# Interleaving two panels on TensorE, with one landing ring of five slots and seven fixed turned slots

## The reference

```python
h = jnp.maximum(_layernorm(x, axis=-1), 0.0)
# the layer, on ego = h (first 2048 rows users, the rest items)
u = par_u[0] * par_u[1] * (diag_u[:, None] * ego_u @ W_u) + ego_u
i = par_i[0] * par_i[1] * (diag_i[:, None] * ego_i @ W_i) + ego_i
e = jnp.concatenate([u, i], axis=0)
h = adj @ (adj.T @ e)
out = (h - mean(h)) * rsqrt(var(h) + 1e-5) * ln_gamma + ln_beta + res   # res = ego
x = x + out
```

## Time and profile before

| | us |
|---|---|
| median of 3 runs | 540.03 (538.85 to 540.18) |
| the profiled execution, its own time | 538.86 |
| its span, first to last instruction | 537.0 |
| busy: TensorE matmul / VectorE / ScalarE / GpSimd | 445.0 / 343.5 / 312.5 / 26.9 |
| DMA: moved, mean rate | 139.43 MB, 260 GB/s |
| mean granted TensorE clock, share of full | 0.93 |

### The profile page before, as it was taken

How to read it: one execution, slowest core, us unless ns; L and a number is a source line. 1 busy time by engine, 2 the same in 40 slices (tenths; PEclk the granted TensorE clock), 3 DMA queues, 4 the chain that set the end, 5 groups by cost and what they waited for, 6 DMA issues and landing times.

```text
span 537.0 us, 5378 instructions
## 1 busy us (share of the span) xinstructions
PE 445.0 (83%) x2108; PEld 179.7 (33%) x2108; DVE 343.5 (64%) x338; ACT 312.5 (58%) x415; POOL 26.9 (5%) x30
## 2 busy tenths in 40 slices
PE   0747554599969989999969799997899898779996
PEld 0313222243423334324423333433343332334433
DVE  2635199473999941499991149999118999701742
ACT  2365830856699924069993207998324699622242
POOL 1011330000000000000000000000000000001132
PEclk9968795899979999999989899998999999799999
DMA  7966109685965979996957699795979968772911
GB/s 222 404 259 264 56 0 379 169 234 165 366 253 214 408 284 206 324 371 253 415 205 281 191 319 372 269 415 206 330 262 315 392 243 338 276 251 63 302 52 59
DMA packets 63112, 139.43 MB, mean 260 GB/s; under 512 B 4208, under 2 KB 37488, under 8 KB 63088
## 3 DMA queue, kind: packets, MB, share of 16 engines
q1 hardware_dynamic: 45360, 123.28, 63.1%
q10 hardware_dynamic: 17728, 15.82, 10.6%
HBM read 137.78 MB, written 1.31 MB: 259 GB/s over the span
## 4 chain that ended last, share of the span: by engine, by line
PE 29%; ACT 22%; DMA 22%; DVE 18%; issue 6%; ACTq 1%; SPq 1%; DVEq 0%
ACT ready L369 20%; DMA nat<-in_adj_dram 17%; PE tT_ps L673 11%; PE h_ps L731 10%; DVE ready L544 8%; DVE ready L533 7%; PE tr_ps L662 5%; DMA ready<-in_adj_dram 3%; DMA diag_sb<-in_L_gnn_diag_i_dram 2%; ACT ready L379 1%; PE tr_ps L710 1%; PE tT_ps L686 1%; ACTq L239 1%; SPq L239 1%; DVE tT_sb L550 1%
## 5 line engine op out<-in xcount | busy, mean ns | idle before, releaser
L369 ACT ACTIVATE ready<-nat 32x1024 f32<-32x1024 f32 x225 | 237.4, 1055 | 65.2 <-PE h_ps L731 47.0
L673 PE MATMUL tT_ps<-nat,e_sb 128*64 128x512 f32 x800 | 199.6, 646 | 31.8 <-DMA nat<-in_adj_dram 28.9
L544 DVE STREAM_TRANSPOSE ready<-ready 128x2048 f32<-128x2048 f32 x80 | 179.5, 2287 | 24.4 <-ACT ready L369 18.2
L731 PE MATMUL h_ps<-ready,t_quads 128*64 128x512 f32 x640 | 178.4, 604 | 7.9 <-DVE ready L544 7.9
L533 DVE COPY ready<-nat 32x1024 f32<-32x1024 f32 x175 | 121.1, 692 | 8.7 <-PE h_ps L731 6.0
L673 PEld LDWEIGHTS tT_ps<-nat,e_sb 128*64 128x64 f32 x800 | 62.1, 147 | 141.4 <-issue 101.8
L731 PEld LDWEIGHTS h_ps<-ready,t_quads 128*64 128x64 f32 x640 | 56.9, 139 | 94.5 <-issue 93.2
L379 ACT ACTIVATE ready<-tr_ps 128x512 f32<-128x512 f32 x80 | 44.0, 595 | 71.9 <-PE tr_ps L662 71.7
L731 PE MATMUL h_ps<-ready,t_blocks 128*64 128x512 f32 x160 | 70.0, 593 | 0.7 <-DVE t_blocks L554 0.7
L662 PE MATMUL tr_ps<-ident,nat 128*128 128x128 f32 x320 | 49.0, 302 | 15.2 <-ACT ready L379 15.2
L662 PEld LDWEIGHTS tr_ps<-ident,nat 128*128 128x128 f32 x320 | 38.6, 154 | 47.4 <-issue 27.9
(11 more groups left out here) (54 smaller groups left out, 118.8 us busy)
## 6 DMA issues: line engine op xcount, KB each, us to landing
nat<-in_adj_dram SPq DMA_DIRECT2D x50, 2048.0 KB, 9.6
ready<-in_adj_dram SPq DMA_DIRECT2D x30, 512.0 KB, 10.3
ready<-in_adj_dram ACTq DMA_DIRECT2D x30, 512.0 KB, 10.5
x_sb<-in_x_dram SPq DMA_DIRECT2D x5, 256.0 KB, 8.7
out_dram<-x_sb SPq DMA_DIRECT2D x10, 128.0 KB, 1.8
ready<-in_L_gnn_W_u_dram SPq DMA_DIRECT2D x2, 16.0 KB, 10.1
ready<-in_L_gnn_W_i_dram SPq DMA_DIRECT2D x2, 16.0 KB, 9.3
gamma_sb<-in_L_gnn_ln_gamma_dram ACTq DMA_DIRECT2D x1, 32.0 KB, 2.6
```

The costliest lines, as they stand in the source:

```text
L369: last = nc.scalar.activation(dst, src, ACT.Copy)
L544: last = nc.vector.transpose(part, part)
L673: last = nc.tensor.matmul(tT_ps[half * D:(half + 1) * D, :], e_sb[:, g * RB + r, :], nat_slot(p, g)[:, r, half * BANK:(half + 1) * BANK], ...
L731: last = nc.tensor.matmul(h_ps[k][half * D:(half + 1) * D, :], t[:, b, :], tile, start=(p == 0 and b == 0), stop=True, skip_group_check=True)
```

## The change

- **Kinds**: three groups are read (0, 5, 8), six moved (1, 2, 3, 4, 6, 9), one turned (7). ScalarE's share of a moved group's 16 blocks is now set for each group.
- **Slots**: `landing` is one ring of five slots through which every transfer goes, natural and second, in the order of the list `LOADS`. `kept` has one fixed slot for each of the seven groups that are not read. In the first panel groups 5 and 6 land in the still empty kept slots of groups 6 and 9 (`EARLY`). A second read stays in its landing slot until its bank of h is summed.
- **TensorE's order**: banks of h of panel p alternate with groups of t of panel p + 1. The groups of t have the same order 0 to 9 in every panel.
- **t out of PSUM**: ScalarE makes both copies (`take_quads`, `take_blocks`), and `turn_t(0)` stands in `finish_t`, ahead of the first bank.
- **Prologue**: two units of x are loaded first, natural loads behind the W loads; the moves of group 1 on ScalarE are cut into three parts between the units, VectorE's stand behind all units.
- **Epilogue**: GpSimd builds `c_blk` in the landing slot of group 9 and so waits for the last moves; `norm_h(0)` stands behind all turns.

```diff
-    KIND = ("read", "move", "read", "move", "read", "move", "turn", "move", "turn", "move")
+    KIND = ("read", "move", "move", "move", "move", "read", "move", "turn", "read", "move")
-    BANKS = ((1, 3), (5, 7), (6, 9), (0, 8), (2, 4))
-    H_ORDER = (1, 3, 5, 7, 9, 6, 8, 0, 2, 4)
-    NATURAL = 4
-    TURNED = 8
-    ACT_MOVES = 9
+    BANKS = ((2, 4), (0, 1), (3, 6), (5, 9), (7, 8))
+    LANDING = 5
+    ACT_MOVES = {1: 8, 2: 10, 3: 9, 4: 8, 6: 8, 9: 10}
+    EARLY = {5: 6, 6: 9}
+    LOADS = [(0, g, False) for g in range(GROUPS) if g not in EARLY]
+    for p in range(PANELS):
+        LOADS.append((p, READS[0], True))
+        if p < LAST:
+            LOADS += [(p + 1, 0, False), (p + 1, 1, False), (p + 1, 2, False)]
+        LOADS.append((p, READS[1], True))
+        if p < LAST:
+            LOADS.append((p + 1, 3, False))
+        LOADS.append((p, READS[2], True))
+        if p < LAST:
+            LOADS += [(p + 1, g, False) for g in range(4, GROUPS)]
...
+        def wait_landing_free(eng, p, g, second):
+            n = LOADS.index((p, g, second)) - LANDING
+            if n >= 0:
+                p0, g0, second0 = LOADS[n]
+                if second0:
+                    eng.wait_ge(h_summed, h_count(p0, g0))
+                else:
+                    eng.wait_ge(t_summed, t_count(p0, g0))
+                    if KIND[g0] == "move":
+                        eng.wait_ge(moved_act, move_count(p0, g0))
+                        eng.wait_ge(moved_dve, move_count(p0, g0))
+                    if KIND[g0] == "turn":
+                        eng.wait_ge(tr_filled, tile_count(p0) + BLOCKS)
...
 # ScalarE
             for p in range(PANELS):
+                take_quads(p)
+                turn_back(p, 3)
+                take_blocks(p)
+                if p == 0:
+                    move(0, 6)
+                move(p, 9)
+                second(p, READS[1])
                 if p < LAST:
+                    move(p + 1, 1)
+                second(p, READS[2])
...
 # VectorE
             for p in range(PANELS):
+                if p == 0:
+                    move(0, 6)
+                move(p, 9)
+                turn_read(p, READS[0])
+                turn_moved(p, 6)
+                turn_moved(p, 9)
...
 # TensorE
+            for p in range(PANELS - 1):
+                sum_h(p, 0)
+                sum_h(p, 1)
+                sum_t(p + 1, 0)
+                sum_t(p + 1, 1)
+                sum_h(p, 2)
+                sum_t(p + 1, 2)
+                sum_t(p + 1, 3)
+                sum_h(p, 3)
+                sum_t(p + 1, 4)
+                sum_h(p, 4)
+                sum_t(p + 1, 5)
+                sum_t(p + 1, 6)
+                turn_tiles(p + 1, 0)
+                sum_t(p + 1, 7)
+                turn_tiles(p + 1, 1)
+                sum_t(p + 1, 8)
+                sum_t(p + 1, 9)
+                finish_t(p + 1)
```

More of the change, by code:

```diff
@@ L72, in sem @@
             return ctx.enter_context(nc.semaphore(name))
-        nat = sb("nat", [P, NATURAL, SLOT])
-        ready = sb("ready", [P, TURNED, SLOT])
+        landing = sb("landing", [P, LANDING, SLOT])
+        kept = sb("kept", [P, len(KEPT), SLOT])
         x_sb = sb("x_sb", [P, ALL_BLOCKS, D])
@@ L136, in gnn_layer_kernel, with kept_slot, landing_slot @@
         pstep = sem("pstep")
[L139 to L149, removed]
+        def kept_slot(g):
+            return kept[:, KEPT.index(g), :]
+        def landing_slot(p, g, second):
+            return landing[:, LOADS.index((p, g, second)) % LANDING, :]
@@ new lines, in wait_kept_free @@
+        def wait_kept_free(eng, p, g):
+            if p:
+                eng.wait_ge(h_summed, h_count(p - 1, g))
+                return
+            if g in (TURN, KEPT[-1]):
+                eng.wait_ge(e_ready, PAIRS)
+            for g0, at in EARLY.items():
+                if at == g:
+                    eng.wait_ge(t_summed, t_count(0, g0))
+                    if KIND[g0] == "move":
+                        eng.wait_ge(moved_act, move_count(0, g0))
+                        eng.wait_ge(moved_dve, move_count(0, g0))
@@ L273, in _ @@
                     sp.dma_start(w_blk[half * D:(half + 1) * D, s, half * D:(half + 1) * D], W[:, :]).then_inc(w_in, 16)
-            for u in range(1, PAIRS):
+            natural(0, 0)
+            for u in range(2, PAIRS):
                 load_x(u)
-            for g in FIRST_ORDER[1:]:
+            for g in range(1, GROUPS):
                 natural(0, g)
@@ L431, in _ @@
                     second(p + 1, READS[0])
-                    turn_back(p + 1, HELD[0] - 1)
+                    turn_back(p + 1, 0)
+                    move(p + 1, 6)
+                    turn_back(p + 1, 1)
                     take_tT(p + 1)
-                    for batch in HELD:
-                        turn_back(p + 1, batch)
+                    turn_back(p + 1, 2)
             def squares_h(k):
@@ L611, in norm_h @@
                     scaled_rows(k, tr_ps[k % 2], half, rows64(work(k % 2))).then_inc(out_normed, 1)
-            turn(LAST, READS[0])
-            norm_h(0)
-            turn(LAST, READS[1])
-            turn(LAST, READS[2])
-            for k in range(1, PAIRS - 1):
+            turn_read(LAST, READS[1])
+            turn_read(LAST, READS[2])
+            for k in range(PAIRS - 1):
                 norm_h(k)
@@ L655, in turn_tiles @@
             def turn_tiles(p, batch):
-                g, first = BATCHES[batch]
-                for b in range(first, first + BATCH):
-                    n = tile_count(p, g) + b
+                pe.wait_ge(natural_in[TURN], 16 * (p + 1))
+                for b in range(batch * BATCH, (batch + 1) * BATCH):
+                    n = tile_count(p) + b
                     if n >= 2:
@@ L733, in sum_h, with sum_e @@
                 last.then_inc(h_summed, 1)
+            def sum_e(g):
+                if g % 2 == 0:
+                    pe.wait_ge(e_ready, g // 2 + 1)
+                sum_t(0, g)
             pe.wait_ge(ident_ready, 1)
```

321 lines of the change are left out of this document (156 added, 165 removed).

## The result

The changed kernel takes 483.41 us (median; 479.45 to 485.20), the kernel before 540.11 in the same comparison (538.85 to 541.48): a ratio of 0.894 with a 95% interval of 0.887 to 0.901. The forecast was 472, with a range of 458 to 498: the time lies in the range and 11 us above the forecast.

The account below looks back on a forecast made before the run. ScalarE's moves, crowded into the half panel of t, were taken as the bound. Start 92, first period 88.8, three periods 231.6, tail 56.1 made 468.5; 1.9 outside the span and 1.2 to the median gave 471.6, said 472, range 458 to 498.

Parts of the forecast that it names:

- The mechanism: Whole period: ScalarE's moves crowd into the half panel of t; interleaving h and t hides them, period 92.7 to 77.2 us.
- The rival by which only the removed transposes and the start count: All periods: interleaving does not fill the waits, only removed transposes and the start gain; 505 us, chance 3%.
- TensorE's part of a period: Each period: TensorE's work 75.2 us with one turned group less, plus a wait of 0.5 in finish_t.
- Start, first period: Up to the second panel's t: start 92 us against 115.5, first period 88.8 against 93.5.
- VectorE's chain: Start: last unit some 3 us behind 50.6, then 29 blocks (20.3) and four turns (18), also giving 92 us.
- slot-9 chain: First period: VectorE writes kept slot 9 only after ScalarE moves group 6 out; bank (0, 1) waits 11 us, 2.1 lower clock.
- The tail: After the last sum_t: hT_copy(0) late on ScalarE, a wait of 3.3 and 2.1 of clock; 56.1 us against 50.7.
- Natural loads of groups 8 and 9: Ahead of sum_t 9: two loads beside ScalarE's half of the next second read; wait 0 to 4 us, 1.5 taken.
- three signs of being wrong: Trace: TensorE waits for natural loads elsewhere (groups 3 or 6), bank (0, 1) waits in every panel, or period over 80.
- main case: Whole kernel: forecast 472 us, own range 460 to 484, period between 75.7 and 80; chance 73%.
- DMA-bound ring: Every period: all transfers pass one ring, delays don't heal; period 80 to 86, 499 us at 84; chance 15%.
- slower rival: Ring in lockstep: each of 13 loads issued only after the one before lands, 100 us per panel, 551 us; chance 3%.

Follow-up runs that it names:

- strict order: Changed kernel with TensorE back in the earlier order, five banks of h, then ten groups of t, loads and turns following: 616.51 us, 1.144 times the kernel before.
- kinds alone: Kernel before with only group 6 moved instead of turned, TensorE's order kept: 565.02 us, 1.047 times the kernel before.
- new start: Changed kernel with group 8 landing early in kept slot 9, group 6 moved ahead of take_tT(0), group 3's turn behind read 0's: 472.85 us.
- full-width run: Changed kernel with each second read one 2 MB DMA over 128 partitions from SP's queue, h of read groups not the reference's: 463.81 us, 0.859.
- crosswise deal: Changed kernel with group 8 early in kept slot 9, moves and turns reordered, SP reading quadrants 0, 2 and ScalarE 3, 1: 487.53 us, 0.904.

## Why the prediction was right, and where it was wrong

**The mechanism: right.** The strict order loses 78 us, the kinds alone 26; all together gain 57, 32.5 of it in the start. The rival by which only the removed transposes and the start count is out: alone the removed transposes gain nothing, and the three middle periods fell by 9.7 us each, where 4.1 of transposes went. No run gives the interleaving by itself, with the slots of before.

**TensorE's part of a period: right.** 75.2 and a wait of 0.5 in `finish_t` were worked out; a period takes 75.1, the wait of 0.48 in it, when nothing is late (one DMA per second read). That is 0.6 less than forecast.

**Start, first period: the sum right, its parts not, and in part by luck.** TensorE was through at 83, not 92, since ScalarE ended the units' work at 43.3 for 52: I took the two whole moves out of the 61.3 of the earlier trace rows and put eight blocks back in at full price, but three at a time they fit between the units. VectorE's chain, which I gave as 92 too, ended at 89.2; TensorE does not need its turns 3 and 4 for the last `sum_t`, but `take_tT(0)` stands behind them, and so the gain came back as a wait of 6.6. The wait ahead of bank (0, 1) measured 9.8 for 11. That the sum comes out at 181.3 for 180.8 is luck beyond this: VectorE's chain ended 2.8 us earlier than forecast, and from one turn of t to the next the first period lost 16.4 us to waits and a lower clock, where 13.1 were forecast. The run with the new start bears out the slot-9 chain: without it that wait is gone. The wait ahead of the turn of t stays, at 7.7 us for 6.6.

**The tail: right to 2 us.** 53.9 for 56.1: TensorE waits 2.75 us for `hT_copy(0)`, where 3.3 were forecast, and no lower clock follows (PEclk 1.00 in the tail). That is this execution's: with one DMA per second read, the batch behind a wait of 2.77 takes 2.05 us instead of 1.13.

**The term that was wrong: "Natural loads of groups 8 and 9", the 1.5 us of the period.** The place is right, group 9 ahead of the end of `sum_t`, and the size is wrong: 4.16, 3.90 and 4.20 us of wait, the upper end of the 0 to 4 from which 1.5 was chosen, and 1.7 to 3.0 of lower clock behind each, where the term had none. I priced two loads and a half by the best stretches of the trace, 392 and 328 GB/s, with at most a remainder of one load ahead of them. In fact the DMA engines never catch up: the middle periods run at 325 to 343 GB/s with a share above 1, and 27.26 MB at that rate is 80 to 84 us.

The number that says so stood in the earlier trace rows: share times period was 75 to 80 us before, beside TensorE's 75.2. It belonged in the sum as a bound beside TensorE's work, and I used it only in a rival. It even grew, to 83 to 86 (1.04 x 81.7, 1.02 x 84.3, 1.01 x 82.2), as more transfers run side by side; in the packet records of the whole kernel a 4 KB packet went from a mean 170 to 177 ns, a 1 KB packet from 57 or 58 to 61 on ScalarE's queue and 66 on SP's.

Where the time goes can be split by the packets. The full-width run moves 364 GB/s at a share of 0.94, so an estimated 387 at a full share, near the 392 of the earlier trace rows; its 13 loads take 70.1 us of packet time per period. In the changed kernel it is 84.0: the ten natural loads take 59.0 instead of the 53.9 that is theirs of the 70.1, and the 6.29 MB of second reads 25.0 instead of 16.2, which is 252 GB/s. So about two thirds of the 13.9 us is what the second reads cost themselves, and one third is what they cost the natural loads beside them (217 ns a packet for 167). The best stretch was the price of natural loads that fly alone.

**The prediction's own signs.** Of the three signs of being wrong that it lists, one came out clearly, all three middle periods over 80 us, and one barely, 0.53 us of wait at group 3. ScalarE's longest idle stretch in a middle period was to be under 5 us and is 9.6, behind tiles of `turn_tiles`. The total still came out near, since the tail was 2.2 us shorter and start and first period cancelled: 483.4 lies 0.6 us inside the 460 to 484 of the main case, whose period was to be 80 at most. So the narrower range held by luck, and the wider one, which allows for the DMA-bound case, for the reason that it gives.

**The rivals.** The DMA-bound ring (15%) told the period, 80 to 86, rightly; its 499 is too high because it charged 6.8 us on all four periods, where only the three middle ones had it, at 5.5 each. The argument against it, 392 GB/s, held for natural loads flying alone only. The Trainium skill's per-core limit of about 358 GB/s (DMA: Bandwidth & Descriptors, Specifications) isn't what binds: the full-width run holds 364 over three periods and still isn't bound by it. The round-robin rule that the prediction took from the Trainium skill (DMA: Bandwidth & Descriptors, Queues, rings and completion order), by which the half shares with groups 8 and 9, did point the right way, at 1.5 or more, and the trace agrees: 217 ns for a natural packet beside a second read, 167 without. The slower rival fell for this kernel. The strict order, with periods of 115 to 125 us, is slower than it, but not by its lockstep: there TensorE waits for a second read, up to 21.4 us in one stretch.

**What stays open.** The expectation for the crosswise deal missed, and its explanation is untested. Which part of the full-width read's 20 us comes from the 128 partitions, which from one DMA instead of four and which from one queue, no run shows; nor does one show whether the deal of the quadrants acts where they are written or where they are read. A full-width read that brings the blocks into the places that the turns want was not tried; nor was a ring with another number of slots, or the interleaved order with the slots of before. Why 4 KB runs over 32 partitions are slower than 1 KB runs was measured, not explained.

The best version that computes the whole is the one with the new start, 472.85 us: 0.875 [0.870, 0.880] of the kernel before, and 2% under the changed kernel.

## What to carry to other kernels

Before the gain of an overlap is added up, put busy share times period of every engine side by side, the DMA engines among them: that product is a warning near the period that you forecast, and it is no constant (75 to 80 us before, 83 to 86 after), and a best stretch's GB/s is not a price for transfers of another shape or in other company. Where two engines meet within a few us, the three reorderings tried here only moved the wait or made transfers dearer; fewer or cheaper bytes removed it. A change that is worth much as a whole can hold parts that are a loss alone, as the ring without the interleaved order (+78 us) and the kinds (+26 us) here, so test the parts before you keep or drop one.

## What the runs showed that was not expected

- A 2 MB read over 128 partitions instead of four over 32 takes 20 us off this kernel (463.81 for 483.41 to 484.28), at the same bytes, though with the blocks not in the places that the turns want.
- Which queue carries which quadrant of a second read is worth 13 to 15 us (497.52 and 487.53 against 484.28 and 472.85), with no other instruction changed.
- A natural load's 4 KB packet takes 167 ns while no second read is in flight, and 217 while one is (middle periods of the changed kernel).
- 4 KB runs to 32 partitions are slower than 1 KB runs: +25 and +12 us.
- With 1.05 MB less per period, the DMA share stays at 1.01 to 1.03 while TensorE waits for a load for 1.0 us at most: a share near 1 alone doesn't say that an engine waits, and the chain of waits is needed beside it.
